# Two cross attentions of a decoder: the small products of one group of samples issued at other steps of the loop

## The reference

```python
x = x + _L0_attn_ref(_layernorm(x), ...)      # 16 heads of 64
x = x + _L0_xattn_ref(_layernorm(x), ctx_512, ...)   # 16 heads of 16
x = x + _L0_ffn_ref(_layernorm(x), ...)
x = x + _L1_attn_ref(_layernorm(x), ...)
x = x + _L1_xattn_ref(_layernorm(x), ctx_512, ...)   # 16 heads of 64
x = x + _L1_ffn_ref(_layernorm(x), ...)       # 64 experts, 8 a token
```

## Time and profile before

| | |
|---|---|
| median of 3 runs | 3632.3 us (3623.47 to 3633.61) |
| profiled execution | 3628.8 us, its span 3627.0 us |
| PE busy | 3279.1 us (90%) |
| DVE busy | 1890.2 us (52%) |
| ACT busy | 1664.0 us (46%) |
| POOL busy | 783.1 us (22%) |
| first cross attention | from about 641 to 1282 us |
| second cross attention | from about 2160 to 3230 us |

### The profile page before, as it was taken

How to read it: one execution, slowest core, us unless ns; L and a number is a source line. 1 busy time by engine, 2 the same in 40 slices (tenths; PEclk the granted TensorE clock), 3 DMA queues, 4 the chain that set the end, 5 groups by cost and what they waited for, 6 DMA issues and landing times. The chain is left out here.

```text
span 3627.0 us, 76508 instructions
## 1 busy us (share of the span) xinstructions
PE 3279.1 (90%) x24554; PEld 2430.0 (67%) x24555; DVE 1890.2 (52%) x5145; ACT 1664.0 (46%) x4616; POOL 783.1 (22%) x854
## 2 busy tenths in 40 slices
PE   5999998899999979899997979999999999979982
PEld 4777776566666656677775756767767777756761
DVE  3555555577777756222223644565655656653333
ACT  2555554566666621122221326666666666631220
POOL 0000000000000000333332110223323233234773
PEclk9999999899999989999998989999999999999996
DMA  8400000300000041211112010100000000114774
GB/s 271 133 0 0 0 0 13 136 8 10 10 8 10 6 140 50 65 31 30 29 25 54 0 50 7 30 28 20 18 9 15 13 11 13 43 48 113 219 203 126
DMA packets 141202, 181.21 MB, mean 50 GB/s; under 512 B 36156, under 2 KB 115001, under 8 KB 140108
## 3 DMA queue, kind: packets, MB, share of 16 engines
q1 hardware_dynamic: 89890, 134.89, 12.1%
q0 software_dynamic: 45760, 26.67, 4.6%
q10 hardware_dynamic: 5482, 18.73, 1.4%
HBM read 116.11 MB, written 103.61 MB: 61 GB/s over the span
## 5 line engine op out<-in xcount | busy, mean ns | idle before, releaser
L1247 DVE TENSOR_REDUCE e_nmx<-PS 128x1 f32<-128x361 f32 x416 | 221.3, 532 | 397.9 <-PE PS L1093 349.6
L1594 ACT ACTIVATE b_p<-PS,b_nmx 100x361 f32<-100x361 f32 x512 | 275.2, 568 | 163.4 <-DVE b_nmx L1681 163.4
L1093 PE MATMUL PS<-e_cT,e_qT 128*128 128x361 f32 x832 | 336.0, 486 | 0.0
L882 POOL DMA_INDIRECT slot_rows<-r_row,r_rows_now x256 | 256.3, 1001 | 360.4 <-DVE e_p L1254 306.0
L1198 ACT ACTIVATE e_pT<-PS 121x384 f32<-121x384 f32 (+1 forms) x416 | 198.6, 478 | 219.7 <-PE PS L1100 214.0
L1681 DVE TENSOR_REDUCE b_nmx<-PS 100x1 f32<-100x361 f32 x512 | 247.6, 526 | 90.7 <-PE PS L1442 88.8
L2587 PE MATMUL PS<-c_wgu,c_tile_xT 128*128 x912 | 290.2, 461 | 1.4 <-ACT c_tile_xT L2642 1.4
L1100 PEld LDWEIGHTS PS<-ident,e_p 128*121 128x121 f32 x1248 | 198.5, 185 | 102.2 <-ACT e_pT L1198 6.6
L1203 ACT ACTIVATE e_p<-PS,e_nmx 128x361 f32<-128x361 f32 x416 | 232.3, 559 | 36.3 <-DVE e_nmx L1247 36.2
L1449 PE MATMUL PS<-ident,b_p 100*121 100x100 f32 x1536 | 222.3, 281 | 6.6 <-PEq L191 4.2
L2587 PEld LDWEIGHTS PS<-c_wgu,c_tile_xT 128*128 128x128 f32 x912 | 169.6, 191 | 78.2 <-issue 3.3
(11 more groups left out here) (339 smaller groups left out, 6491.9 us busy)
## 6 DMA issues: line engine op xcount, KB each, us to landing
f_w<-in_f_W SPq DMA_DIRECT2D x64, 384.0 KB
slot_rows<-a_empty SPq DMA_DIRECT2D x1, 21504.0 KB, 64.9
f_xg<-slot_rows SPq DMA_DIRECT2D x64, 336.0 KB
c_wgu<-in_c_GU ACTq DMA_DIRECT2D x8, 1408.0 KB, 16.6
sum<-X SPq DMA_DIRECT2D x2, 3200.0 KB, 57.3
f_sums<-sum SPq DMA_DIRECT2D x16, 400.0 KB
b_cT<-in_ctx_T SPq DMA_DIRECT2D x32, 181.5 KB, 2.3
e_cT<-in_ctx_T SPq DMA_DIRECT2D x32, 181.5 KB, 2.4
```

The costliest lines, as they stand in the source:

```text
L882: pool.indirect_dma_start(out=self.rows, in_=self.row[:, u, :], in_offset=None, out_offset=bass.IndirectOffsetOnAxis(ap=self.rows_now[:, u ...
L1093: sr.fill_done(pe.matmul(sr.at(f"s{m}", ROWS, CTX), qT[:, at:at + ROWS], cT[:, u, 0:CTX], start=True, stop=True), f"s{m}")
L1247: dve.tensor_reduce(nmx[:, m:m + 1], sr.at(f"s{m}", ROWS, CTX), AX.X, ALU.max, negate=True).then_inc(max_ready, 1)
L1594: sr.move_done(act.activation(p[:, g % 2, a, 0:CTX], sr.at(f"s{g}{a}", S, CTX), ACT.Exp, bias=nmx[:, g, a:a + 1]), f"s{g}{a}")
```

## The change

Second cross attention: queries 2 and 3 are issued at steps 17 and 18 (before 19 and 21), value product v0.0 at step 10 (before 17), v0.1 to v0.3 at steps 19, 20 and 21, one a step; VectorE adds y0 at step 13 (before 14), ahead of the part of `choose` of that step. The order of banks 6 and 7 follows.

First cross attention: one piece of a step is issued right behind its scores, the other between the two halves of its transposes. The pieces are dealt to the steps anew, and bank 7's order with them. ScalarE copies the first piece between exponentials 0 and 1 and the second ahead of exponential 3 (`move_probs(…, 0)` behind exponential 1, `move_probs(…, 2)` last); `move_queries(1)` comes ahead of exponential 0 of step 3. VectorE does the first piece's part ahead of maximum 3, and layer norm statistics at step 2 and its application at step 3 (before both at 2). The opening ahead of the loop is put in the same order (left out below, as are the loops that follow from `V0_AT` holding one number a step). One doubled wait on `loaded` goes.

```diff
@@ -910,8 +910,8 @@
     Y_AT = {13: 0, 24: 1}
     X_AT = 4
     P_AT = {5: 0, 7: 1, 11: 2, 12: 3}
-    Q_AT = {14: 0, 15: 1, 19: 2, 21: 3}
-    V0_AT = {17: (0,), 18: (1, 2), 20: (3,), 23: (4,), 25: (5,)}
+    Q_AT = {14: 0, 15: 1, 17: 2, 18: 3}
+    V0_AT = {10: 0, 19: 1, 20: 2, 21: 3, 23: 4, 25: 5}
     V1_AT = {0: 0, 1: 1, 2: 2, 4: 3, 6: 4, 8: 5}
     ROUTED_X, ROUTED_L, ROUTED_C = 8, 10, 17
     CHOOSE_AT = (12, 13, 14, 15, 16, 18, 19, 20)
@@ -948,7 +948,7 @@
         routed = {"rx": ROUTED_X, "rl": ROUTED_L, "rc": ROUTED_C}
         order = [(X_AT, 0, "xT")] + [(n, 1, f"p{j}") for n, j in P_AT.items()]
         order += [(n, 2, f"q{r}.{j}") for n, j in Q_AT.items() for r in range(HT)]
-        order += [(n, 3, f"v0.{m}") for n, ms in V0_AT.items() for m in ms]
+        order += [(n, 3, f"v0.{m}") for n, m in V0_AT.items()]
         led = [name for _, _, name in order]
         order += [(n, 4, name) for n, name in own.items()] + [(n, 5, name) for name, n in routed.items()]
         mr = Ring(k, 6, 2).plan([name for _, _, name in sorted(order)]).ends(TURNS, [*own.values(), *routed])
@@ -1284,7 +1282,7 @@
                         if nxt and n == 8:
                             mr.wait_full(dve, "xT", i + 1)
                             apply(i + 2)
-                        if this and n == 14:
+                        if this and n == 13:
                             dve.wait_ge(biased, i * 2 + 2)
                             add(0, i)
                         if prev and n in CHOOSE_AT:
@@ -1349,8 +1350,8 @@
         sr = Banks(k, 0, 4).plan([f"s{g}{a}" for g in range(GROUPS) for a in range(TILES_R)])
         tr = Banks(k, 4, 2).plan([f"p{g}{a}" for g in range(GROUPS) for a in range(TILES_R)])
         ob = Banks(k, 6, 1).plan(["o0", "o1"])
-        mr = Ring(k, 7, 1).plan(["v10", "v12", "xT", "r0", "t0", "q", "k00", "y0", "v00", "k01", "v02", "r1",
-                                 "t1", "k10", "y1", "k11"])
+        mr = Ring(k, 7, 1).plan(["v10", "v12", "xT", "k00", "r0", "q", "t0", "k01", "y0", "v00", "v02", "k10",
+                                 "r1", "k11", "t1", "y1"])
         mr.ends(TURNS, ["v10", "v12", "r0", "t0", "y0", "r1", "t1", "y1"])
 
         def ahead(n, by, i, this, nxt):
@@ -1493,6 +1494,24 @@
                         at = ahead(n, AHEAD, i, this, nxt)
                         if at:
                             scores(*at)
+
+                        if this and n == 0:
+                            values(1, 0, i)
+                        if nxt and n == 1:
+                            turn_x(i)
+                        if this and n == 2:
+                            turn_sums(0, i)
+                        if this and n == 3:
+                            turn_out(0, i)
+                        if this and n == 4:
+                            out(0, i)
+                        if nxt and n == 5:
+                            values(0, 2, i)
+                        if this and n == 6:
+                            turn_sums(1, i)
+                        if this and n == 7:
+                            turn_out(1, i)
+
                         at = ahead(n, WEIGHED, i, this, nxt)
                         if at:
                             weigh(*at)
@@ -1502,64 +1521,50 @@
                             turn_probs(at[0], 1, at[1])
 
                         if this and n == 0:
-                            values(1, 0, i)
+                            values(1, 2, i)
                         if nxt and n == 1:
-                            turn_x(i)
-                        if this and n == 2:
-                            turn_out(0, i)
+                            keys(0, 0, i)
+                        if nxt and n == 2:
+                            queries(i)
                         if nxt and n == 3:
-                            keys(0, 0, i)
-                        if nxt and n in (4, 5):
-                            values(0, 2 * (n - 4), i)
-                        if this and n == 6:
-                            turn_out(1, i)
+                            keys(0, 1, i)
+                        if nxt and n == 4:
+                            values(0, 0, i)
+                        if nxt and n in (5, 6):
+                            keys(1, n - 5, i)
                         if this and n == 7:
                             out(1, i)
 
                         if at:
                             turn_probs(at[0], 2, at[1])
                             turn_probs(at[0], 3, at[1])
-
-                        if this and n == 0:
-                            values(1, 2, i)
-                        if this and n == 1:
-                            turn_sums(0, i)
-                        if nxt and n == 2:
-                            queries(i)
-                        if this and n == 3:
-                            out(0, i)
-                        if nxt and n == 4:
-                            keys(0, 1, i)
-                        if this and n == 5:
-                            turn_sums(1, i)
-                        if nxt and n in (6, 7):
-                            keys(1, n - 6, i)
 
...
@@ -1606,60 +1610,56 @@
                 def turn(i, this, nxt):
                     for n in range(GROUPS):
                         at, before = ahead(n, AHEAD, i, this, nxt), ahead(n, TURNED, i, this, nxt)
-                        if at:
-                            exponent(at[0], 0, at[1])
                         if nxt and n == 3:
                             sr.wait_full(act, f"s{GROUPS - 1}{TILES_R - 1}", i)
                             move_queries(1, i)
+                        if at:
+                            exponent(at[0], 0, at[1])
+                        if nxt and n == 1:
+                            move_x(i)
+                        if this and n in (3, 7):
+                            move_out(n // 4, i)
+                        if this and n in (1, 5):
+                            move_sums(n // 4, i)
+                        if at:
+                            exponent(at[0], 1, at[1])
                         if before:
                             move_probs(before[0], 0, before[1])
-                        if this and n == 1:
-                            move_sums(0, i)
-                        if this and n == 5:
-                            move_sums(1, i)
                         if at:
-                            exponent(at[0], 1, at[1])
                             exponent(at[0], 2, at[1])
                         if nxt and n == 1:
-                            move_x(i)
-                        if this and n == 2:
-                            move_out(0, i)
+                            move_keys(0, 0, i)
+                        if nxt and n == 2:
+                            move_queries(0, i)
                         if nxt and n == 3:
-                            move_keys(0, 0, i)
-                        if this and n == 6:
-                            move_out(1, i)
+                            move_keys(0, 1, i)
+                        if nxt and n in (5, 6):
+                            move_keys(1, n - 5, i)
+                        if at:
+                            exponent(at[0], 3, at[1])
                         if before:
                             move_probs(before[0], 2, before[1])
-                        if at:
-                            exponent(at[0], 3, at[1])
-                        if nxt and n == 2:
-                            move_queries(0, i)
-                        if nxt and n == 4:
-                            move_keys(0, 1, i)
-                        if nxt and n in (6, 7):
-                            move_keys(1, n - 6, i)
 
...
-                def norm(t):
-                    xs = [X[:, 2 * t + u, :] for u in range(2)]
-                    norm_statistics(dve, ln, Chain(norm_step, LN_STEPS), t, xs)
-                    norm_apply(dve, ln, t, xs)
+                def statistics(t):
+                    norm_statistics(dve, ln, Chain(norm_step, LN_STEPS), t, [X[:, 2 * t + u, :] for u in range(2)])
+
+                def apply(t):
+                    norm_apply(dve, ln, t, [X[:, 2 * t + u, :] for u in range(2)])
 
                 def turn(i, this, nxt):
                     for n in range(GROUPS):
@@ -1709,32 +1710,35 @@
                         if at:
                             for a in range(3):
                                 maximum(at[0], a, at[1])
+                        if this and n == 0:
+                            move_values(1, 0, i)
+                        if this and n in (2, 6):
+                            divide(n // 4, i)
+                        if this and n == 4:
+                            add(0, i)
+                        if nxt and n == 5:
+                            move_values(0, 2, i)
+                        if at:
+                            maximum(at[0], 3, at[1])
                         if before:
                             move_probs(before[0], 1, before[1])
```

(77 more changed lines are left out.)

## The result

The changed kernel is slower: 3679.0 us (median of 4 runs, 3675.3 to 3682.6) against 3628.5 of the kernel before on the same chip (4 runs, 3623.5 to 3633.6), a ratio of 1.0139 [1.0122, 1.0155]. I had forecast 3644 with a range up to 3660. The direction was right; the size was not, and the time lies outside the range.

What follows compares the result with a forecast made beforehand. TensorE was taken to bound both cross attentions, so reordering wins back only its waits. From 3628.8, -13 for the first and +25 for the second gave 3640.8; 3.5 for the runs' median made 3644 us, range 3618 to 3660.

Steps and rivals of the forecast that it cites:

- (d): Second cross attention, steps 15 to 19: TensorE's clock falls to 1.2 GHz, adding 112 us, 3756 in all; chance 0.02.
- Second cross attention, what moves: Second cross attention: waits of 1.03, 1.84 and 1.76 replace old ones; a turn costs 1.85 us more, +25 us overall.
- 0.70 if VectorE were not late: Second cross attention, step 17: the positions product's wait for the query copy, 1.84 us, would be 0.70 with VectorE in time.
- The 1 us that I let the turn without routing win: Second cross attention: the first turn, which has no routing, gains about 1 us.
- the term -13: First cross attention: a turn falls from 39.07 to 38.2 us, 0.86 less; with last turn and prologue, -13 us.
- The new waits: First cross attention: scores wait 0.36 to 0.44, transposes 0.35, step 3's query copy chain 0.75; 3.01 us a turn.
- I take nothing: First cross attention: changed spacings between neighbouring products add about 0.5 us a turn and give about 0.5 back, net nothing.
- B + 1.55: First cross attention: TensorE reaches the next scores 1.55 us after B, the start of a step's second piece, a key product.
- (a): First cross attention: the last exponential doesn't hold the scores up, so 29 us go, 3615 in all; chance 0.13.
- (b): Second cross attention: VectorE catches up, only waits without lateness stay, 3614 at the limit; chance 0.25 together with (c).
- (c): Both cross attentions: the stages cancel or waits only change places, 3632 us; chance 0.25 together with (b).
- +11 and +38: Upper bounds: first cross attention, unbalanced spacings and extra 0.2 for eight pieces, +11; second, each wait larger by 0.3, +38.

Runs made afterwards that it cites:

- experiments 2: Changed kernel with query products 0 and 2 done twice and step 18's transposes repeated, results unchanged: 3613.6 us, 1.0018 of the kernel before.
- (3): Changed kernel repeating only query product 0: 3657.8 us, 1.0132 of the kernel before; repeating only query product 2 and step 18's transposes: 3614.6 us, 1.0017.
- experiment 5: Changed kernel with VectorE's add put back from step 13 to step 14: 3622.9 us, 1.0052 of the kernel before.
- Experiment 4: Changed kernel with VectorE's add of step 13 behind the routing's part, not ahead of it: 3621.9 us, 1.0045 of the kernel before.
- experiment 7: New first cross attention with ScalarE's fourth exponential ahead of its second piece's copy, second stage as before: 3561.5 us, 0.9887 of the kernel before.
- half kernels (1): Kernel before with only the first cross attention's change: 3582.8 us, 0.9936; with only the second's: 3682.0 us, 1.0214.

## Why the prediction was wrong

**The step that failed** is rival (d), "the clock falls", with its chance of 0.02. I took the full clock in turns with waits of 1.22 and 0.80 as evidence that three waits of 1.0, 1.8 and 1.8 would keep it too. The rows told nothing of waits that long, and so close: in the changed kernel 4.3 us lie between the starts behind the second and the third. With the range's upper end at 3660 the case was left out altogether. The mechanism was as (d) has it, at about the place it names, but smaller than its price: 6.8 to 10.2 us at the lower level, the third wait among them, cost 3.06 a turn and not 8. Over the 13 whole turns that is 13 x 3.06 = 40 us; the added idle time over the same turns, 13 x 1.82 = 24. With the full clock and everything else as measured, 3682.6 would have been some 3643 or a little less, inside the forecast's own range. Shown by the filled waits (experiments 2 and 3), and by turns of equal idle time in one kernel (5). Either of the two later waits can be the one at which it falls (3). What a gap must be for the clock to fall, and why it falls in one turn and not in the next with the same waits, stays open.

The Trainium skill (TensorE: Matmul & The Clock Gate, A second HAM failure mode: psum-queue depth-cycling) tells of short idle gaps of TensorE between groups of products, in a bf16 kernel with 512 columns that cycles through the PSUM banks, which bring the clock down again and again. The trace agrees: three waits for a bank, none over 1.66 us, brought it down in 13 of 13 whole turns, for 40 us. I had set the rule aside because the kernel before has gaps too.

**Second cross attention, what moves.** Places, order and releasers of the three waits were right, and the sum (1.85 a turn more, measured 1.82 of idle time; turn of 67.6, measured 67.54 with the clock kept and the gaps filled). That the sum fits so well is in part luck. The single waits of 1.84 and 1.76 were 0.24 and 0.41 too large; part of the 1.35 is hidden because the products ahead of it run at the lower clock: at full clock it is 1.66 (experiments 4 and 5, and four turns of the changed kernel), so that the three waits are 4.31 and not 4.63. Against that I had counted 0.50 for late restarts and spacings that go, and at full clock the busy time falls by only 0.22 (63.45 to 63.23, experiment 5). The limit "0.70 if VectorE were not late" was right with the add at 14 (0.70) but not with the add at 13 behind the maxima (1.42): there VectorE is still late. Experiment 4's expectation failed on that. The 1 us that I let the turn without routing win did not come: 5.9 were lost ahead of the first positions product, the first two waits and query product 2, which now stands ahead of it, among them.

**First cross attention.** The mechanism was right, the term -13 mis-sized: -22.6 in the profile, -24.5 alone. A turn gained 39.07 - 37.88 = 1.19 and not 0.86, which makes 18 over 15 turns; the opening, which I let pay 1, won 4.6 (its first loop turn's scores begin at 668.64, before at 673.23). The new waits were of the forecast size, if anything larger: four scores held up by 0.43 to 0.45 (forecast 0.36 to 0.44), the scores and the query chain of step 3 together 1.32 (1023.70 to 1025.82, less 0.80; forecast 0.39 + 0.75), 0.2 ahead of a transpose (0.35), together some 3.3 against 3.01. What I missed is thus on the side of the gains: by 39.07 - 3.87 + 3.3 = 38.5 the turn should have been 0.6 longer than it is. "I take nothing" for the spacings is the step that was too careful, and the timelines of the two turns show it. Start to start, with the listed idle times taken off, the sixteen groups of transposes took 12.69 us before and 11.64 after, the four key products 3.14 and 2.94: 1.25 less, where the forecast has 0.25 (0.6 for old waits less 0.35 for the new one). The 0.84 for transposes ahead of scores is from the opening; in the turn after they cost 0.71 there (1028.14 to 1028.85, experiment 7), and a key product ahead of transposes 0.63 (1027.51 to 1028.14) and not 0.71. So TensorE reaches the scores at B + 1.34, not B + 1.55, and with the measured 0.45 the bank is free at B + 1.79, not B + 1.91: two errors that nearly cancel in the wait.

**The rivals.** (a) fell: the last exponential does hold the scores up, and the order that frees it first won 18 us (7). (b) fell: VectorE does not catch up within steps 13 to 17. (c) fell with the half kernels (1): -24.5 and +74.7 do not cancel.

**The range** did not follow from its own terms. The limits of (a) and (b) are 3615 and 3614, not 3618, and the two upper bounds, +11 and +38, would together give 3632 + 49 = 3681, not 3660. That 3679 lies just below this sum is chance: the +38 stands for larger waits at full clock, and the second stage's waits were smaller than forecast. A smaller slip: in the second stage ScalarE and VectorE are idle for 38 and 39% of a turn, which is more than the third that I named.

## What to carry to other kernels

A wait of TensorE costs its length only as long as the clock holds; where a change makes waits longer than any that the trace shows at full clock, or brings two of them close together, the fall belongs in the forecast with a real chance, and the busy time of equal stretches at equal product counts tells the two parts apart. Filling such a gap with idle products is a cheap test of it, and here also a partial cure. An instruction that waits should stand behind independent work on its engine, not ahead of it, and a copy that only starts the next piece behind the operation that frees a bank.

## What was not expected of the hardware

With waits of 1.05, 1.60 and 1.35 to 1.66 us the granted clock went from 1.00 to 0.50 for 6.8 to 10.2 us in each of 13 whole turns, in nine of them before the third wait had begun, while with 1.04, 0.91 and 1.00 it never did, and with 1.21, 0.70 and 1.66 it did in eight turns of 13. Repeating products, with no result used from the repetition, made the second stage's turn shorter: 67.5 us with 14 to 22 more products against 70.6 without.
